# A fused attention kernel: coefficient steps and V in single places, the exchange of maxima in a scores bank, a subtraction in front of both maxima

## What is computed

```python
def conv_ref(x, Wq, Wk, Wv, gamma):      # x here is the group-normalised input
    xf = x.reshape(B, C, -1)
    f = einsum('qc,bcn->bqn', Wq, xf)     # 64 channels
    g = einsum('qc,bcn->bqn', Wk, xf)     # 64 channels
    h = einsum('vc,bcn->bvn', Wv, xf)     # 256 channels
    scores = einsum('bqn,bqm->bnm', f, g)
    beta = softmax(scores, axis=1)        # over n
    o = einsum('bvn,bnm->bvm', h, beta)
    return gamma[0] * o + xf
def gn(v, G=32, eps=1e-5): ...            # group norm over 8 channels x 4096 pixels
out = x + conv_ref(gn(x), Wq, Wk, Wv, gamma)
```

## Time and profile before

| | |
|---|---|
| median of three executions | 2012.44 us (2009.02 to 2014.24) |
| the profiled execution, its own time | 2015.34 us |
| its span in the profile | 2013.6 us |
| mean granted TensorE clock | 0.985 |
| PE busy | 1915.7 us (95%) |
| DVE busy | 1661.2 us (83%) |
| ACT busy | 1591.8 us (79%) |
| POOL busy | 1312.0 us (65%) |

### The profile page before, as it was taken

One profiled execution on the slowest core, in us unless ns is written; L12 is line 12 of the kernel. 1 busy time (PEld: TensorE's weight loads), 2 busy tenths in 40 slices (PEclk: granted clock), 3 DMA queues, 4 the chain that ended last, 5 costly groups with the idle time before them and its releaser, 6 DMA issues. The chain is left out here.

```text
span 2013.6 us, 44173 instructions
## 1 busy us (share of the span) xinstructions
PE 1915.7 (95%) x17476; PEld 1567.4 (78%) x17476; DVE 1661.2 (83%) x2021; ACT 1591.8 (79%) x1699; POOL 1312.0 (65%) x746
## 2 busy tenths in 40 slices
PE   2889999999999998999999999999999999999998
PEld 1578877887778886888777887788867788888887
DVE  7779888988868889898876889899887688888884
ACT  3588878888868886888876887788887688888885
POOL 3067666885646765787553766588755576777776
PEclk9899999999999998999999999999999999999999
DMA  3012211211102221121110221122111111111111
GB/s 108 12 31 73 72 33 40 72 33 22 49 19 60 56 74 28 50 68 31 45 27 17 71 73 53 21 70 53 32 33 27 28 22 32 31 31 32 32 30 35
DMA packets 193628, 86.97 MB, mean 43 GB/s; under 512 B 149136, under 2 KB 186256, under 8 KB 193424
## 3 DMA queue, kind: packets, MB, share of 16 engines
q1 hardware_dynamic: 193424, 84.16, 15.8%
HBM read 46.60 MB, written 16.78 MB: 31 GB/s over the span
## 5 line engine op out<-in xcount | busy, mean ns | idle before, releaser
L312 POOL TENSOR_TENSOR PL<-SC,PH 128x1024 f16<-128x1024 f32 x512 | 1095.9, 2147 | 666.6 <-ACT SC L531 664.1
L418 PE MATMUL O<-V,PH 128*128 128x257 f16 x4096 | 1123.0, 274 | 11.5 <-DVE OSB L749 6.3
L420 PE MATMUL O<-V,PL 128*128 128x257 f16 x4096 | 1122.2, 274 | 0.0
L419 PE MATMUL O<-V,PH 128*128 128x256 f16 x4096 | 1120.8, 274 | 0.0
L530 ACT ACTIVATE PH<-SC 128x1024 f16<-128x1024 f32 x512 | 540.0, 1055 | 132.9 <-PE O L420 119.3
L524 ACT ACTIVATE SC<-S 128x1024 f32<-128x1024 f32 x512 | 502.6, 1013 | 150.4 <-issue 133.2
L713 DVE TENSOR_TENSOR SC<-SC,MB 128x1024 f32<-128x1024 f32 x512 | 614.7, 1210 | 0.2
L677 DVE TENSOR_TENSOR XM<-S,XM 128x1024 f32<-128x1024 f32 x384 | 468.2, 1219 | 151.6 <-PE S L406 149.7
L531 ACT ACTIVATE SC<-SC 128x1024 f32<-128x1024 f32 x512 | 533.7, 1042 | 0.0
L418 PEld LDWEIGHTS O<-V,PH 128*128 128x128 f16 x4096 | 407.8, 100 | 64.8 <-DVE OSB L749 10.7
L419 PEld LDWEIGHTS O<-V,PH 128*128 128x128 f16 x4096 | 402.4, 98 | 51.5
(11 more groups left out here) (81 smaller groups left out, 1138.7 us busy)
## 6 DMA issues: line engine op xcount, KB each, us to landing
xin<-x SPq DMA_DIRECT2D x24, 1024.0 KB, 5.7
xres<-x SPq DMA_DIRECT2D x64, 256.0 KB, 2.9
out<-RES SPq DMA_DIRECT2D x64, 256.0 KB, 2.2
ATT<-OT SPq DMA_DIRECT2D x1008, 16.0 KB, 1.8
SC<-x SPq DMA_DIRECT2D x4, 1024.0 KB, 8.5
GG<-GG SPq DMA_DIRECT2D x32, 128.0 KB, 2.6
SC<-wvT SPq DMA_DIRECT2D x1, 256.0 KB, 9.6
SC<-wqT SPq DMA_DIRECT2D x2, 64.0 KB, 10.6
```

Of the source, the lines that this page charges most:

```text
L312: pool.tensor_tensor(PL[:, s % RING, :], sc(s), PH[:, s % RING, :], ALU.subtract).then_inc(pl_ready, 1)
L418: mm(o[:, 0:C + 1], PH[:, n % RING, cols], vh, start=t == 0, stop=False)
L419: mm(o[:, 0:C], PH[:, n % RING, cols], vl, start=False, stop=False)
L420: w = mm(o[:, 0:C + 1], PL[:, n % RING, cols], vh, start=False, stop=t == T - 1)
```

## The change

- The small steps of the coefficients are cut into five functions, at (chunk, group) (5, 3), (5, 5), (5, 7), (6, 3) and (6, 5). The group means `gmean`, the inverse roots `gr` and two differences lie in the PSUM tile MB instead of SBUF. A Newton step multiplies in another order; there are 23 steps instead of 22.
- Statistics and normalisation of the next batch's input are halved over groups 3 and 5, and ScalarE's rounding over groups 4 and 6. In the prologue each half is released singly.
- F and G stand at the end of groups 0 to 6 of chunk 13 and of group 0 of chunk 14. V stands at the end of groups 0 to 6 of chunk 15, and in nine places of chunk 0.
- The fold is gone. XM is turned whole (128x1024) in group 7 (`turn_maxima`), and `quadrant_maxima` reduces it over two dimensions in group 1.
- The exchange matmul goes to the first scores bank, in the middle of group 3, and waits for both stores and both maxima of group 2; the scores of group 4 wait for `column_maxima`. The waits for it in front of projections are gone.
- In even groups VectorE subtracts first, then takes both maxima.

```diff
-        [(FG_FIRST, g, END) for g in (0, 1, 3, 4, 5, 6)] + [(FG_FIRST + 1, g, END) for g in (0, 1)])}
-    V_AT = {place: i for i, place in enumerate(
-        [(CPB - 1, 0, END)] + [(CPB - 1, g, e) for g in (1, 3, 4, 5, 6) for e in (MID, END)])}
+        [(FG_FIRST, g, END) for g in range(7)] + [(FG_FIRST + 1, 0, END)])}
+    V_AT = {place: i for i, place in enumerate([(CPB - 1, g, END) for g in range(7)])}
     V_LATE = {place: len(V_AT) + i for i, place in enumerate(
-        [(0, 0, END), (0, 1, MID), (0, 1, END), (0, 3, MID), (0, 3, END)])}
+        [(0, 0, END), (0, 1, MID), (0, 1, END), (0, 2, END), (0, 3, MID), (0, 3, END), (0, 4, END),
+         (0, 5, MID), (0, 5, END)])}
...
+        gmean = MB[:, M + 32:M + 32 + NG]
+        gr = MB[:, M + 64:M + 64 + NG]
+        gd = MB[:, M + 96:M + 96 + 32].rearrange("p (a b) -> p a b", a=NG)
+        gd2 = MB[:, M + 128:M + 128 + 32].rearrange("p (a b) -> p a b", a=NG)
...
-                    pe.wait_ge(mxc_ready, k + (2 if g > 2 else 1))
...
+                    if g == 4:
+                        pe.wait_ge(mxc_ready, k + 2)
                     scores(n + 2 * G)
...
-                if g == 2 and k + 1 < K:
-                    pe.wait_ge(osb_ready, MB2 * k)
-                    if j == FG_FIRST and b + 1 < BATCH:
-                        pe.wait_ge(fg_done, (b + 1) * NFG + 2)
-                    if j == FG_FIRST + 1 and b + 1 < BATCH:
-                        pe.wait_ge(fg_done, (b + 2) * NFG)
-                    if j == CPB - 1:
-                        pe.wait_ge(v_done, (b + 1) * NV + 3)
-                    if j == 0 and b > 0:
-                        pe.wait_ge(v_done, b * NV + len(V_AT) + 3)
-                    share_maxima(k + 1, spare(k))
+                if g == 3 and k + 1 < K:
+                    read = min(n + 2 * G + 1, K * G)
+                    pe.wait_ge(s_stored, read)
+                    pe.wait_ge(s_maxed, read)
+                    share_maxima(k + 1, S[:, 0, :])
...
+                if g in (4, 6) and b + 1 < BATCH and NORM_FIRST <= j < NORM_FIRST + NPC:
+                    p, h = j - NORM_FIRST, g // 2 - 2
+                    act.wait_ge(xn_ready, H * ((b + 1) * NPC + p) + h + 1)
+                    nc.scalar.copy(XH[:, h, piece(p)], xin[:, h, :]).then_inc(xh_ready, 1)
...
+            def group_variances(n):
+                step = stepper(n, 5)
+                spread = gmean.unsqueeze(2).to_broadcast([P, NG, GN])
                 ve.tensor_copy(bm[:, :, :], spread)
-                step(ve.tensor_tensor(tm[:, :, :], tm[:, :, :], spread, ALU.subtract))
-                step(ve.tensor_tensor(tm[:, :, :], tm[:, :, :], tm[:, :, :], ALU.mult))
-                step(ve.tensor_tensor(tv[:, :, :], tv[:, :, :], tm[:, :, :], ALU.add))
+                step(ve.tensor_tensor(gd, tm[:, :, :], spread, ALU.subtract))
+                step(ve.tensor_copy(tm[:, :, :], gd))
+                step(ve.tensor_tensor(gd2, tm[:, :, :], gd, ALU.mult))
+                step(ve.tensor_tensor(tv[:, :, :], tv[:, :, :], gd2, ALU.add))
                 step(ve.tensor_reduce(gvar[:, :], tv[:, :, :], axis=AX.X, op=ALU.add))
                 step(ve.tensor_scalar(gvar[:, :], gvar[:, :], 1.0 / GN, EPS, ALU.mult, ALU.add))
-                assert done[0] == COEF_VAR
-
-            def inverse_roots(n):
-                step, done = stepper(n, COEF_VAR)
-                flat = "p a b -> p (a b)"
+
+            def newton(step):
+                step(ve.tensor_tensor(gt[:, :], gvar[:, :], gr, ALU.mult))
+                step(ve.scalar_tensor_tensor(gt[:, :], gt[:, :], -0.5, gr, ALU.mult, ALU.mult))
+                step(ve.scalar_tensor_tensor(gr, gt[:, :], 1.5, gr, ALU.add, ALU.mult))
+
+            def guess_roots(n):
...
+            def turn_maxima(c):
+                dve.wait_ge(s_maxed, G * (c + 1))
+                if c > 0:
+                    dve.wait_ge(mxq_ready, c)
+                ve.transpose(MT[:, :], XM[:, :]).then_inc(mx_turned, 1)
+
             def quadrant_maxima(c):
 
-                dve.wait_ge(mx_ready, c + 1)
-                ve.transpose(MT[:, :], MX[:, :]).then_inc(mx_turned, 1)
                 dve.wait_ge(mx_turned, c + 1)
-                ve.tensor_reduce(mxq, MT[:, :].rearrange("p (j n) -> p j n", j=NB), axis=AX.X,
+                ve.tensor_reduce(mxq, MT[:, :].rearrange("p (i j n) -> p j i n", i=GT, j=NB), axis=AX.XY,
                                  op=ALU.max).then_inc(mxq_ready, 1)
...
-                if g % 2 == 0 and k + 2 < K:
-                    maximum(n + 2 * G + 1)
                 if n + SUB_LEAD < K * G:
                     subtract(n + SUB_LEAD)
                 if g % 2 == 0 and k + 2 < K:
+                    maximum(n + 2 * G + 1)
                     maximum(n + 2 * G)
                 if g == 7 and k + 2 < K:
-                    fold_maxima(k + 2)
+                    turn_maxima(k + 2)
                 if g == 1 and k > 0:
                     turn_blocks(k - 1)
...
-                    column_maxima(k + 1, spare(k))
+                    column_maxima(k + 1, S[:, 0, :])
...
+                        for h in range(H):
+                            last = ve.bn_stats(stats[:, h, 2 * p + part, :], xin[:, h, part * 512:(part + 1) * 512])
+                        if part == 1:
...
+                        normalise(xin[:, part, :], part).then_inc(xn_ready, 1)
+                if b + 1 < BATCH:
+                    if (j, g) == (COEFS_AT, 3):
+                        dve.wait_ge(xin_read, (b + 1) * NPC)
+                        group_means(b + 1)
+                    if (j, g) == (COEFS_AT, 5):
+                        group_variances(b + 1)
+                    if (j, g) == (COEFS_AT, 7):
+                        guess_roots(b + 1)
+                    if (j, g) == (COEFS_AT + 1, 3):
+                        finish_roots(b + 1)
+                    if (j, g) == (COEFS_AT + 1, 5):
+                        spread_coefficients(b + 1)
```

More of the change, by code:

```diff
@@ L44, in groupnorm_attention @@
     STAT_FIRST = 1
-    VARS_AT = 5
-    ROOTS_AT = 6
+    COEFS_AT = 5
     NORM_FIRST = 7
@@ L113, in groupnorm_attention @@
         tv = sb("tv", [P, NG, GN], f32)
-        gmean = sb("gmean", [P, NG], f32)
         gvar = sb("gvar", [P, NG], f32)
-        gr = sb("gr", [P, NG], f32)
         gt = sb("gt", [P, NG], f32)
@@ L588, in _ @@
                 extra(k, g, END)
-                if g == 6 and b + 1 < BATCH and NORM_FIRST <= j < NORM_FIRST + NPC:
-                    p = j - NORM_FIRST
-                    act.wait_ge(xn_ready, (b + 1) * NPC + p + 1)
-                    for h in range(H):
-                        nc.scalar.copy(XH[:, h, piece(p)], xin[:, h, :]).then_inc(xh_ready, 1)
+                if g in (4, 6) and b + 1 < BATCH and NORM_FIRST <= j < NORM_FIRST + NPC:
+                    p, h = j - NORM_FIRST, g // 2 - 2
+                    act.wait_ge(xn_ready, H * ((b + 1) * NPC + p) + h + 1)
+                    nc.scalar.copy(XH[:, h, piece(p)], xin[:, h, :]).then_inc(xh_ready, 1)
         @block.vector
@@ L599, in stepper @@
             def stepper(n, before):
-                done = [before]
+                done = [n * COEF + before]
                 def step(ins):
@@ L604, in step, with group_means @@
                     ins.then_inc(coef_step, 1)
-                    dve.wait_ge(coef_step, n * COEF + done[0])
-                return step, done
-            def group_variances(n):
-                step, done = stepper(n, 0)
+                    dve.wait_ge(coef_step, done[0])
+                return step
+            def group_means(n):
+                step = stepper(n, 0)
                 for h in range(H):
@@ L640, in inverse_roots, with finish_roots, spread_coefficients @@
+            def finish_roots(n):
+                step = stepper(n, 16)
+                newton(step)
+                newton(step)
+            def spread_coefficients(n):
+                step = stepper(n, 22)
+                flat = "p a b -> p (a b)"
                 ve.transpose(nmean[:, :], bm[:, :, :].rearrange(flat))
-                step(ve.tensor_copy(br[:, :, :], gr[:, :].unsqueeze(2).to_broadcast([P, NG, GN])))
-                assert done[0] == COEF
+                step(ve.tensor_copy(br[:, :, :], gr.unsqueeze(2).to_broadcast([P, NG, GN])))
@@ L784, in _ @@
                     for h in range(H):
-                        last = normalise(x0[:, h, piece(q)], h)
-                    last.then_inc(xn_ready, 1)
+                        normalise(x0[:, h, piece(q)], h).then_inc(xn_ready, 1)
                 if q > 0:
@@ L840, in _ @@
                 extra(k, g, END)
-                if g == 5 and b + 1 < BATCH:
+                if g in (3, 5) and b + 1 < BATCH:
+                    part = g // 2 - 1
                     if STAT_FIRST <= j < STAT_FIRST + NPC:
@@ L856, in _ @@
                         dve.wait_ge(xin_in, 16 * (2 * NPC * b + NPC + p + 1))
-                        for h in range(H):
```

(4 more changed lines are left out.)

55 lines of the change are left out of this document (19 added, 36 removed).

## The result

The changed kernel takes 1996.47 us (median of four, 1992.35 to 1996.65), against 2013.34 for the kernel before: a ratio of 0.9915, 95% interval 0.9896 to 0.9935. It is faster, by 17 us and not by 54. The profiled execution has a span of 1994.5 us, 19.1 less than before.

A forecast was written before the change was run, and what follows sets the result against it. TensorE bounds ordinary chunks; the time to win lies around batch borders. Gains of 17.2 us per border, 51.6 in three, plus 0.7 and 1.5 make 54: median 1958 us from 2012.4, range 1945 to 1982, own range 1950 to 1970.

The forecast's parts named there:

- What bounds the kernel, and the losses by chunk: Ordinary chunks are pure TensorE at 27.30 us; chunks around batch changes lose 23.7 us per border, 71 in three.
- Part (f): Even groups: subtracting before both maxima ends the second maximum 1.1 us earlier; nothing gained or lost in ordinary chunks.
- Part (a): Coefficient steps in chunks 5 and 6: PSUM and five places leave losses of 1.0 and 0.3 us.
- Part (e): Exchange matmul in a scores bank, group 3: costs nothing unless the reduction exceeds 2.4 us.
- The margin of 0.8 us: Ordinary chunk: second maximum ends at 719.72 after moving earlier, group 3's first half at 720.5, leaving 0.8 us.
- Part (b): Normalisation halved over groups 3 and 5: 0.2 us lost per chunk, 0.8 for four, against 3.0 before.
- the third of the signs: Sign that the prediction is wrong: chunks 7 to 11 remain at 28 us.
- Parts (c) and (d): V, F and G respread in chunks 13 to 0; fold replaced by whole turn and reduction, 0.2 us less VectorE per chunk.
- 358.9: Time in us TensorE needs from chunk 5 to the next batch's chunk 0: twelve chunks plus V, F and G projections.
- the 6.5 that the prediction let stay: Loss in us per border forecast to remain of 23.7, so 17.2 are gained.
- the 2.7 and 1.2 us of chunks 0 and 13: Losses forecast to stay per border: chunk 0 with nine V projections 2.7, chunk 13 with F and G 1.2.
- the locks move along: Rival, chance 0.20: exposed steps still wait for GpSimd, 5 to 8 us more stay per border, 1975 to 1982 us.

The follow-up runs named there:

- the kernels without the gap: Changed kernel with odd maximum, subtraction, even maximum in even groups (1973.6 us), or with ScalarE's even store between the two exponentials (1983.01 us).
- the three points undone: Changed kernel with the old maximum-subtraction-maximum order, the exchange mostly in group 2 and O's spare bank, and gvar's sum and a copy in PSUM: 1961.65 us.
- the fastest one: The 1961.65 us kernel with F and G's last projection moved from group 0 to the end of group 4 of chunk 14: 1958.05 us.
- the order alone: Kernel before with only the even groups' order changed to subtraction, odd maximum, even maximum: 2010.26 us, ratio 0.9986.

## Why the prediction was wrong

*What bounds the kernel, and the losses by chunk:* right. The gains came from the chunks named, and ordinary chunks of the changed kernel stayed at 27.30 us. What the sum left out is the clock: it reckoned with 1.00 everywhere, and at 0.95 five chunks lost 1 to 2 us each.

*Part (f), the subtraction in front of both maxima:* this step failed. I wrote that the second maximum "ends 1.1 us earlier" and that VectorE's lateness costs nothing there. It waits for ScalarE's even store, which is in the code and was not in my reckoning: in the ordinary chunk it starts after 0.54 us of idle time and ends 0.3 us earlier. Where VectorE is late, the odd maximum is 1.1 us later and ScalarE's odd store with it, and all that ScalarE and GpSimd do behind it. Undoing it is worth 22.9 us, the largest of the three. Of this chunks 8 to 11 give 9.5 us, chunk 6 8.0, chunk 14 5.5 and chunk 13 3.6, and ordinary chunks take some back; the part of chunk 14 is mostly clock.

*Part (a), the coefficients:* PSUM frees the steps, as said. I named the steps that stay exposed, the two on gvar among them, and priced the whole at 1.3 us per border for chunks 5 and 6; they are 3.6 to 4.8, and 13.3 us in three borders go when the two leave SBUF. The size was off: both waits come in every batch, 1.5 us each, and the second stands in front of the division.

*Part (e), the exchange in a scores bank:* right for ordinary chunks (no wait at all), wrong where VectorE is late. The margin of 0.8 us was reckoned in an undisturbed chunk, where it is 0.55, and used for all. The exchange stands half a group ahead of the scores, so the same lateness costs TensorE earlier: 16 us by the run that moved it back, much of which overlaps with the other two or is the normalisation's place and the clock.

*Part (b), the normalisation:* 0.8 per border forecast, 3.8 measured, and 0.0 in the kernels without the gap or with the exchange moved. Its mean duration was the 1.7 us that I took, but as a mean of 2.6 in group 3 and 0.8 in group 5. That chunks 8 to 11 stay at 28.0 to 28.4 is the third of the signs that it named for itself.

*Parts (c) and (d):* chunk 15 at 36.5 and chunk 0 at 41.85 us, as written (36.5 and 41.8). Chunk 13 lost 2.0 instead of 1.2, from (f). The turn's and reduction's durations were right, but that less VectorE time in a chunk can only help was not: alone they cost 5 us, for what counts is what stands in front of the maxima.

With the three points undone, the first border is 365.4 us, which is 358.9 and the 6.5 that the prediction let stay. That is luck in part: chunks 5 to 7 lose nothing there and chunks 8 to 11 0.1 us, where 2.1 were forecast, and chunk 14 loses 2.5 where 0.5 was. The time is 1961.65 against the 1958 forecast, for another kernel; the 1958.05 of the fastest one says nothing for the forecast either. The prices of the projections and the 2.7 and 1.2 us of chunks 0 and 13 came out. The two new orderings took 30.7 us of the 54 (1996.47 against 1965.74), the two steps on gvar 4.1 more.

The rival *the locks move along* named a part of it (the exposed steps and the normalisation), but its 1975 to 1982 were too low, and it did not name the larger part. No rival named the two engines taking turns on the banks. That the parts do not add (22.9, 16 and 13 alone, 34.8 together) is shown; how the 22.9 divide between the gap, the late odd store, GpSimd's place and the clock is not shown beyond the chunks told above, nor is why the clock fell behind a wait of 2.46 us in two chunks 6 and not in the third.

The Trainium skill (PSUM — Partial Sum Buffer, PSUM bank collisions raise a hardware error) states that two engines must not be on the same partitions of one bank at once, reads included; that is a reason for the store's and the maximum's waits on each other. No run here took such a wait out of the program. Of the lock on the shared ports (SBUF — State Buffer, Who interferes with whom) the rows read here agree: the small steps with a PSUM input average 0.13 to 0.2 us, those on gvar end with GpSimd's instruction.

## What to carry to other kernels

Before an instruction is moved away from between two others, ask what it covers there: a wait that shows nowhere in the profile may lie under it. A margin read in an undisturbed stage holds for that stage; at a place where an engine is known to be late, the wait has to be reckoned with its lateness. A small step that ends only with another engine's instruction is best given an operand elsewhere; moved in the order, it took its wait along here. Where a view names one engine for a wait on several, the ends of all of them have to be read: here it named the store, and the maximum ended last. And when two kernels are compared chunk by chunk, the granted clock and the single durations of what can be blocked come first, for either can be worth more than the edit.

## What the runs showed of the hardware

- The same normalisation of 128x1024 took 0.77 to 0.90 us where GpSimd was not in its way, and 1.97 to 2.62 us where it began early in GpSimd's instruction. Little decides it: 2.62 us when it began 0.06 us after that instruction, 0.77 when it began 0.08 us before. Edits that have nothing to do with it moved the mean (790 ns with the exchange moved, 808 with the order alone, 1713 in the changed kernel).
- A scalar step of 128x4 from PSUM took 133 and 151 ns, the same from SBUF 165 and 170 ns when nothing was in its way (in the kernel before): PSUM was no dearer for it.
- A VectorE turn of 128x1024 took 1238 ns, and a reduction of 1024 to 8 over two dimensions 1190 ns, where the fold of 1024 to 256 over a strided one took 1962.
- Behind a wait of 2.4 to 2.7 us TensorE's granted clock fell to half in five chunks of the changed kernel (0.95 over the chunk), and the chunk grew by 1 to 2 us more than the wait. Behind a wait of 2.46 us in the second chunk 6 it stayed at 1.00.
